# The last stage's fp4 rounding in a transformer layer: constants that need no clamp, and one of GpSimd's three passes given to ScalarE

## The reference

```python
def fp4_quant_dequant(x):
    xb = x.reshape(shape[:-1] + (shape[-1] // BLOCK, BLOCK))
    scale = jnp.maximum(jnp.max(jnp.abs(xb), axis=-1, keepdims=True) / 6.0, 1e-12)
    xn = xb / scale
    idx = jnp.searchsorted(_MID, jnp.abs(xn))   # grid 0, .5, 1, 1.5, 2, 3, 4, 6
    return (_GRID[idx] * jnp.sign(xn) * scale).reshape(shape)
...
gate, y = fp4_linear(x, w_gate), fp4_linear(x, w_up)
h = jax.nn.silu(gate) * y
return fp4_linear(h, w_down)
...
x = _layernorm(x + attention(x)); x = _layernorm(x + ffn(x))
```

## Time and profile before

| what | us |
|---|---|
| median of 3 runs | 3667.35 |
| lowest and highest run | 3665.51, 3670.27 |
| time of the profiled execution | 3665.53 |
| its span | 3663.7 |

### The profile page before, as it was taken

One profiled execution on the slowest core, in us unless ns is written; L12 is line 12 of the kernel. 1 busy time (PEld: TensorE's weight loads), 2 busy tenths in 40 slices (PEclk: granted clock), 3 DMA queues, 4 the chain that ended last, 5 costly groups with the idle time before them and its releaser, 6 DMA issues.

```text
span 3663.7 us, 68990 instructions
## 1 busy us (share of the span) xinstructions
PE 3406.8 (93%) x27752; PEld 1532.9 (42%) x27752; DVE 3389.2 (93%) x3547; ACT 2581.8 (70%) x4818; POOL 944.0 (26%) x1014
## 2 busy tenths in 40 slices
PE   7769999999999999999999999999999969899997
PEld 4433333333333333333333333333333346666665
DVE  8898999999999999999999999999999659999997
ACT  4442888888888888888888888888888922222332
POOL 6881000010000000000000000000000038888887
PEclk9885999999999999999999999999999989999999
DMA  5452122211211111111111111111111111211100
GB/s 162 144 175 82 57 68 72 78 64 67 72 56 46 58 66 68 49 43 49 49 57 59 67 59 41 41 50 58 66 58 61 38 43 59 64 45 39 40 31 19
DMA packets 134508, 230.63 MB, mean 63 GB/s; under 512 B 29510, under 2 KB 84006, under 8 KB 121894
## 3 DMA queue, kind: packets, MB, share of 16 engines
q1 hardware_dynamic: 124972, 217.82, 17.6%
q10 hardware_dynamic: 9216, 8.39, 0.7%
HBM read 156.33 MB, written 68.16 MB: 61 GB/s over the span
## 4 chain that ended last, share of the span: by engine, by line
PE 72%; DVE 17%; issue 4%; ACT 3%; POOL 2%; DMA 1%; SPq 1%; ACTq 0%; DVEq 0%; POOLq 0%
PE ps L625 36%; PE ps L678 32%; PE ps L758 3%; DVE arena L974 2%; DVE arena L979 1%; DVE arena L1128 1%; DVE v_all L1113 1%; DVE arena L1105 1%; ACT arena L842 1%; DVE arena L1118 1%; PE ps L665 1%; ACT arena L851 1%; DVE arena L967 1%; DVE v_all L1171 1%; DVE v_all L1123 1%
## 5 line engine op out<-in xcount | busy, mean ns | idle before, releaser
L997 DVE TENSOR_REDUCE arena<-ps 128x1 f32<-128x1024 f32 x2048 | 2495.4, 1222 | 113.5 <-PE ps L625 96.8
L851 ACT ACTIVATE arena<-ps 128x512 f32<-128x512 f32 x4096 | 2226.1, 597 | 357.8 <-PE ps L665 272.8
L625 PE MATMUL ps<-kst,qst 48*128 48x512 f32 x4096 | 1518.6, 451 | 28.1 <-DMA qst<-qk_parts 23.8
L665 PE MATMUL ps<-qst,kst 51*128 51x512 f32 x4096 | 1490.6, 447 | 0.0
L678 PE MATMUL ps<-arena 128*32 128x256 f32 x16384 | 1308.6, 392 | 71.1 <-ACT arena L842 67.2
L625 PEld LDWEIGHTS ps<-kst,qst 48*128 48x128 f32 x4096 | 613.5, 187 | 884.8 <-DVE arena L997 719.4
L678 PEld LDWEIGHTS ps<-arena 128*32 128x32 f32 x16384 | 326.2, 108 | 795.7 <-issue 456.8
L1252 POOL TENSOR_TENSOR arena<-arena,ones 128x16 bf16<-128x16 f32 x64 | 14.2, 222 | 2425.8 <-DVE arena L1002 2425.8
L665 PEld LDWEIGHTS ps<-qst,kst 51*128 51x128 f32 x4096 | 605.0, 185 | 11.1 <-ACT arena L851 7.7
L899 ACT ACTIVATE v_all<-ps 128x352 f32<-128x352 f32 x128 | 59.3, 463 | 315.6 <-PE ps L758 315.6
L758 PE MATMUL ps<-wgT,arena 128*128 128x352 f32 x512 | 203.4, 480 | 38.4 <-ACT arena L882 38.4
(11 more groups left out here) (103 smaller groups left out, 2290.2 us busy)
## 6 DMA issues: line engine op xcount, KB each, us to landing
qk_parts<-arena SPq DMA_DIRECT2D x32, 1024.0 KB, 7.4
kst<-qk_parts SPq DMA_DIRECT2D x128, 256.0 KB
qst<-qk_parts SPq DMA_DIRECT2D x128, 256.0 KB
kst<-qk_parts SPq DMA_DIRECT2D x128, 128.0 KB
qst<-qk_parts SPq DMA_DIRECT2D x128, 128.0 KB
att<-arena SPq DMA_DIRECT2D x256, 34.0 KB
arena<-in_xT SPq DMA_DIRECT2D x16, 512.0 KB, 8.2
arena<-in_x SPq DMA_DIRECT2D x32, 256.0 KB
```

What stands on the lines that cost most here:

```text
L625: mm = nc.tensor.matmul(ps[:, i % S_BANKS, :], q[SROW:SROW + STACK, qt * P:(qt + 1) * P], k[SROW:SROW + STACK, kc * CHUNK:(kc + 1) * CHUNK ...
L665: nc.tensor.matmul(ps[:, bank_of_t(g.c, i), :], kst[g.u % 2][first:first + ROWS, kb * P:(kb + 1) * P], qst[g.u % 2][first:first + ROWS, qb ...
L851: nc.scalar.activation(pt[kb % 2][:, qb * CHUNK:(qb + 1) * CHUNK], ps[:, bank_of_t(g.c, i), :], ACT.Exp).then_inc(p_ready, 1)
L997: nc.vector.tensor_reduce(mx[g.u % 2][:, i // 2, i % 2:i % 2 + 1], ps[:, bank:bank + 2, :].rearrange("p b t -> p (b t)"), AX.X, ALU.max).t ...
```

## The change

The amount that rounds a value now comes from VectorE's two bit operations with another constant (`TO_LARGE`) and lacks a constant part, `STEADY`, that is added by whoever uses it. With that the clamp from below is gone. VectorE adds STEADY in `round_x` and `round_h`, which stay single instructions (`add` and `add` in place of `max` and `add`). ScalarE forms amount plus STEADY into buffers of its own, in two new functions: `steady_x`, 256 columns, and `steady_h`, 704 columns. Both stand behind `store_out` and ahead of `silu` in its list. GpSimd keeps the subtraction and the product, and waits for VectorE's rounding and for ScalarE's amount. For h it waits once ahead of both halves.

```diff
-POWER_BITS, TO_ROUND = 0x40800000, 0x0B400000
+POWER_BITS, TO_LARGE = 0x40800000, 0x0B200000
+STEADY = 1.25 * 2.0 ** 22
...
+            def steady_x(n):
+                act.wait_ge(x_power, n.times(1, 1))
+                nc.scalar.activation(xs_r[n.u % 2], xm_r[n.u % 2], ACT.Identity, bias=steady[:, 0:1]).then_inc(x_steady, 1)
+
+            def steady_h(n):
+                act.wait_ge(h_power, n.times(1, 1))
+                nc.scalar.activation(hs_r[n.u % 2], hm_r[n.u % 2], ACT.Identity, bias=steady[:, 0:1]).then_inc(h_steady, 1)
...
-                (7, silu), (9, hT_out_of_psum)])
+                (6, steady_x), (8, steady_h), (7, silu), (9, hT_out_of_psum)])
...
-                nc.vector.scalar_tensor_tensor(out=hh_r[n.u], in0=hm_r[n.u % 2], scalar=ROUND, in1=hh_r[n.u],
-                                               op0=ALU.max, op1=ALU.add).then_inc(hq_step, 1)
+                nc.vector.scalar_tensor_tensor(out=hh_r[n.u], in0=hm_r[n.u % 2], scalar=STEADY, in1=hh_r[n.u],
+                                               op0=ALU.add, op1=ALU.add).then_inc(hq_step, 1)
...
-            def rounded(t, m, sc, step, at, done, blocks):
+            def rounded(t, steady, sc, step, at, done, blocks):
...
-                nc.gpsimd.tensor_scalar(m, m, ROUND, None, ALU.max).then_inc(step, 1)
-                pool.wait_ge(step, at[0])
-                nc.gpsimd.tensor_tensor(t, t, m, ALU.subtract).then_inc(step, 1)
-                pool.wait_ge(step, at[1])
+                nc.gpsimd.tensor_tensor(t, t, steady, ALU.subtract).then_inc(step, 1)
+                pool.wait_ge(step, at)
                 nc.gpsimd.tensor_tensor(v, v, sc.unsqueeze(2).broadcast_to([P, blocks, BLK]), ALU.mult).then_inc(done, 1)
...
             def round_h(n):
                 p, nb = n.u % 2, FH // BLK
+                pool.wait_ge(hq_step, n.times(1, 1))
+                pool.wait_ge(h_steady, n.times(1, 1))
                 for hf in range(2):
```

More of the change, by code:

```diff
@@ L284, in layer_kernel @@
         xh_r = [take(C) for _ in range(4)]
-        xm_r = [take(C) for _ in range(2)]
+        xm_r, xs_r = ([take(C) for _ in range(2)] for _ in range(2))
         xhT_r = [take(C, "p (c t) -> p c t", c=CT) for _ in range(2)]
@@ L291, in layer_kernel @@
         bn = take(48, "p (t s) -> p t s", s=6)
-        std, rstd, shift, ln_t, ln_d, sums, var, power = (take(8) for _ in range(8))
+        std, rstd, shift, ln_t, ln_d, sums, var, power, steady = (take(8) for _ in range(9))
         XB, HB = slice(0, C // BLK), slice(C // BLK, C // BLK + FF // BLK)
@@ L298, in layer_kernel @@
         e_r = [v_all[:, (6 + i) * FF:(7 + i) * FF] for i in range(2)]
+        hs_r = [v_all[:, (8 + i) * FF:(9 + i) * FF] for i in range(2)]
         ident_in, wa_in, tab_in, wp_in = (sem(n) for n in ("ident_in", "wa_in", "tab_in", "wp_in"))
@@ L335, in layer_kernel @@
             "q_max", "q_small", "x_scaled", "h_scaled", "x_power", "h_power", "xq_step"))
+        x_steady, h_steady = (sem(n) for n in ("x_steady", "h_steady"))
         xr_step, xh_done, xhT_psum, xhT_out = (sem(n) for n in ("xr_step", "xh_done", "xhT_psum", "xhT_out"))
@@ L860, in _ @@
             out_of_psum(At(0, G - 1))
+            act.wait_ge(b_const, 3)
             def norm1(n):
@@ L1117, in powers_x @@
                 dve.wait_ge(x_scaled, n.times(1, 1))
-                nc.vector.tensor_scalar(xm_r[n.u % 2].bitcast(I32), xh_r[n.u].bitcast(I32), POWER_BITS, TO_ROUND,
+                nc.vector.tensor_scalar(xm_r[n.u % 2].bitcast(I32), xh_r[n.u].bitcast(I32), POWER_BITS, TO_LARGE,
                                         ALU.bitwise_and, ALU.bitwise_xor).then_inc(x_power, 1)
@@ L1122, in powers_h @@
                 dve.wait_ge(h_scaled, n.times(1, 1))
-                nc.vector.tensor_scalar(hm_r[n.u % 2].bitcast(I32), hh_r[n.u].bitcast(I32), POWER_BITS, TO_ROUND,
+                nc.vector.tensor_scalar(hm_r[n.u % 2].bitcast(I32), hh_r[n.u].bitcast(I32), POWER_BITS, TO_LARGE,
                                         ALU.bitwise_and, ALU.bitwise_xor).then_inc(h_power, 1)
@@ L1127, in round_x @@
                 dve.wait_ge(x_power, n.times(1, 1))
-                nc.vector.scalar_tensor_tensor(out=xh_r[n.u], in0=xm_r[n.u % 2], scalar=ROUND, in1=xh_r[n.u],
-                                               op0=ALU.max, op1=ALU.add).then_inc(xq_step, 1)
+                nc.vector.scalar_tensor_tensor(out=xh_r[n.u], in0=xm_r[n.u % 2], scalar=STEADY, in1=xh_r[n.u],
+                                               op0=ALU.add, op1=ALU.add).then_inc(xq_step, 1)
             def round_h(n):
                 dve.wait_ge(h_power, n.times(1, 1))
-                nc.vector.scalar_tensor_tensor(out=hh_r[n.u], in0=hm_r[n.u % 2], scalar=ROUND, in1=hh_r[n.u],
-                                               op0=ALU.max, op1=ALU.add).then_inc(hq_step, 1)
+                nc.vector.scalar_tensor_tensor(out=hh_r[n.u], in0=hm_r[n.u % 2], scalar=STEADY, in1=hh_r[n.u],
+                                               op0=ALU.add, op1=ALU.add).then_inc(hq_step, 1)
             def quantise_xh(n):
@@ L1284, in round_x @@
                 pool.wait_ge(xq_step, n.times(1, 1))
-                rounded(xh_r[n.u], xm_r[n.u % 2], q_sc[n.u % 2][:, XB], xr_step, [n.times(2, k) for k in (1, 2)], xh_done, C // BLK)
+                pool.wait_ge(x_steady, n.times(1, 1))
+                rounded(xh_r[n.u], xs_r[n.u % 2], q_sc[n.u % 2][:, XB], xr_step, n.times(1, 1), xh_done, C // BLK)
             def round_h(n):
                 p, nb = n.u % 2, FH // BLK
+                pool.wait_ge(hq_step, n.times(1, 1))
+                pool.wait_ge(h_steady, n.times(1, 1))
                 for hf in range(2):
                     cols = slice(hf * FH, (hf + 1) * FH)
[L1291 to L1295, removed]
+                    rounded(hh_r[n.u][:, cols], hs_r[p][:, cols], q_sc[p][:, HB.start + hf * nb:HB.start + (hf + 1) * nb], hr_step,
+                            n.times(2, hf + 1), hq_done, nb)
+            nc.gpsimd.memset(power[:, :], -0.5)
+            nc.gpsimd.memset(steady[:, :], STEADY).then_inc(b_const, 1)
             pool.wait_ge(b_const, 3)
```

## The result

The changed kernel takes 3622.14 us (median of 4 runs, 3618.48 to 3626.04), the one before 3666.56 us beside it (3665.51 to 3670.27): a ratio of 0.9877, with a 95% interval from 0.9860 to 0.9894, 44 us less. The prediction had 3645 us: the right direction and the time inside the stated range, but only half of the gain: 22 us were forecast. The profiled execution took 3622.5 us, with a span of 3620.7.

What follows compares the result with a forecast made beforehand. VectorE's work per group, blocked beside GpSimd's passes, was the bound; PE would take over. A group of 38.24 + 1.8 + 0.6 = 40.6 us gave -6, -12 and -4 at the ends, -22: 3645 us, range 3610 to 3672.

Steps and rivals of the forecast that it cites:

- (1): GpSimd, last stage: it loses the clamp, 3.2 us per tile, and keeps 4.9 of 8.1 us.
- (2): VectorE's four changed instructions keep shape and kind, so their cost was taken as 0.
- (3): ScalarE gains two instructions, 0.59 and 0.97 us, 1.6 us per step, hidden by its idle time.
- (4): VectorE's ordinary step: blocks of 1.74 us go, a new one of 0.8 us at round_h comes; 8.5 us, below PE's 9.56.
- (5): Norm group: VectorE's small steps take 3.3 us in place of 2.1, and PE stalls 1.8 us, from 0 to 2.3.
- (6): PE's clock: half clock behind the stall costs 1.8 us in one group in three, so +0.6 us per group.
- PE's floor: Rival, 0.14: small steps slip between GpSimd's passes, the stall is gone, a group is 38.3 us; 3609 us.
- No gain: Rival, 0.20: VectorE stays the bound, a late group stays near 41.2 us; 3663 us.
- stall and clock: Rival, 0.08: all five small steps blocked, stall 2.3 us, PE's clock falls behind each, group 42.3 us; 3671 us.
- ScalarE's queue: Rival, 0.07: PE's output matmuls wait 0.9 us per step for SiLU and copies behind steady_h; group 43.6 us, 3688 us.

Runs made afterwards that it cites:

- the reordered kernel before: Kernel before the change, with ScalarE copying the transposed x ahead of norm1 and norm2 where these wait for a group's small steps: 3669.7 us, ratio 1.0010.
- the run with the copy first: Changed kernel, with ScalarE copying the transposed x ahead of norm1 and norm2 where these wait for a group's small steps: 3618.1 us, ratio 0.9871.

## Why the prediction was half right

**The bound of before, and which one takes over: right.** VectorE's blocked time was the bound (the reordered kernel before gains nothing from a stall removed), PE is the bound after, at its 9.56 us and one stall per group.

**(1), (2), (3), the prices: right.** GpSimd lost 35.5 - 22.9 = 12.6 us per group, 3.2 per tile. VectorE's instructions cost the same. ScalarE's two take 0.51 and 0.88 us where 0.59 and 0.97 were assumed, hidden as said (without them a group is 39.27 us too).

**(4), the blocks move: right in place, both sizes too large.** The 1.74 us went, but they were sums of medians and no average: over the nine late groups VectorE's lengths ahead of round_h fell by 5.6 us per group, 1.4 per step, since one step in four was blocked less. The new block makes round_h 1.30 - 0.96 = 0.34 us longer (0.96 is its length in the kernel before and in the run with h alone, beside the one-input pass; its lowest is 0.89), and not 0.8: in one step the x pass begins at 3244.29, beside the power bits of h, and round_h at 3244.54, so only the rest of the pass is waited for. GpSimd's second x pass is held by round_h in turn (1.15 us, where it took 0.62). Neither is on the path.

**(5), the stall: this is the term that failed.** "3.3 us in place of 2.1" for the small steps measured 2.4. Three of five are blocked, as forecast, but the first for 0.24 us and not 0.9. The working let VectorE begin them 0.05 us behind GpSimd's first pass, as today. With VectorE ahead, it is held at SiLU's second half for 0.55 us once the power has been started, so the small steps begin 3276.36 - 3275.82 = 0.54 us behind the pass, of which more than half is over. The blocks of the three are 0.24, 0.48 and 0.68 us, 1.4 together. The start behind PE's end of gate and up was 3276.36 - 3274.43 = 1.93 (forecast 2.0) and the way from the last step to gate and up 3280.18 - 3278.74 = 1.44 (forecast 1.44). So the stall was 0.76 us, where 1.8 was forecast, and nearly all of the difference is the 0.9 us of the small steps. The forecast added the stall to the group as it stands; the step it sits in is 1.03 us longer, so in the group the term is 1.03 and not 1.8.

**(6), the clock: priced at 0.6, and 0.0.** It hangs on (5). No group's stall of 0.76 was followed by half clock. With a stall of 1.68 us a group took 40.19 at full clock. By the same step a stall of 1.8 makes 40.3 us, not 40.6, if the clock holds there as well; that was not run. The nearest stalls above it lie behind the last whole group: one of 1.91 us is followed by half clock in the run with twice the h part (0.60 from 3569 to 3573), one of 1.92 in the changed kernel is not.

**The sum.** The forecast had -18 us for the groups and -4 for the ends, -22. By the trace the 13 whole groups went from 544.3 us (3041.93 to 3586.19) to 510.8 (3038.61 to 3549.43), 33.4 less; what lies ahead of them went down by 3.3 us and what lies behind by 6.2: -43. The forecast had 15 groups, of which two are not whole in the trace; put with the ends, they make its parts -15 for the 13 whole groups and -7 for the rest, against -33.4 and -9.5. Of the 18.4 us missing in the groups, the stall's term gives 13 x (1.8 - 1.03) = 10.0, the clock's 13 x 0.6 = 7.8, and the 0.4 us that late_job was still to cost in four early groups 1.6; that is the whole, to 1 us of rounding. The ends give 2.5. Attention itself ended 1.1 us later than in the trace of before, and is no part of the gain.

**The rivals.** PE's floor needed the small steps free; they aren't, and its 3609 us came once they were made so (3608.9, with a group of 38.46 where it had 38.3). No gain, stall and clock, and ScalarE's queue didn't come. The last of them is real in one step of four, as the run with the copy first and the doubled instruction show.

**The rule of the Trainium skill** was half borne out. L1072 and L1075, which have two inputs, stand still beside GpSimd's two-input passes until the pass ends, as the Trainium skill says (SBUF — State Buffer, Who interferes with whom). That both L1073 and L1076 get through by starting 0.02 us ahead of a pass agrees with its "whoever issues first". That the one-input clamp blocks a two-input VectorE instruction for its whole length is not what the rows show: L1058 starts 0.05 us behind a clamp of 1.09 us and takes 0.44, and in the trace of before 34 of the 52 L1109 run beside the clamp at their lowest length of 0.42.

## What to carry to other kernels

When two engines block each other, the amount of work taken from one says little: one part of this change (h, 2.2 of the 3.2 us taken from GpSimd) gave nearly all of the gain by itself and the other (x) gave none. Lay the remaining passes on the other engine's timeline from the point at which they are released, and see whether they end ahead of the first instruction that they block. Where a handful of very short instructions gates the next stage, keep long passes out of their way with a wait: here one wait made the small steps 1.4 us shorter and a group 0.8 us.

A stall that disappears from the place where it is seen may only have moved: removed at gate and up, it came back once at VectorE's residual and once at ScalarE's copy. Follow the order of the list behind it before you count it as gain.

## What the hardware showed that was not expected

A block's length depends on where in the other engine's pass the instruction arrives, to 0.02 us: five small steps in one row took 0.41, 0.17, 0.65, 0.85 and 0.17 us, the same ones without passes beside them 0.15 to 0.17. The pattern is stable: over 13 groups each of them keeps its length to 0.04 us.

PE's clock fell to half behind seven of eleven stalls of about 2.5 us and more in the kernel before, behind one of three of 2.52 us in the run with more work on VectorE, and behind five of eleven of 2.35 to 2.57 us in the run with x alone. Behind none of the whole groups' stalls of 0.76, 1.38 and 1.68 us did it fall, but it did behind one of 1.91 us. What picks among the longer ones stays open.

The last stage's first matmul started at 2943.65 us in the changed kernel and between 2938.12 and 2952.06 in the profiled executions of the twelve experiments, all of which leave attention alone. A part of the scatter between executions lies in attention, then, and a few microseconds of the last stage are read more surely as distances in the trace.
